# A decoder block on one core: setup merged, values shared by all heads, low parts two tiles later, and high parts made by a multiplication with an accumulator

## The reference, cut to what matters

```python
# 1. x (1024 x 128) goes through 4 sLSTM layers, each with a small feed-forward part
def step(carry, wx_t):
    h, c, n, m = carry
    raw = wx_t + jnp.einsum('bhd,hdgo->bhgo', h, rk) + b
    ...
    hn = jax.nn.sigmoid(og) * cn / nn
_, ys = lax.scan(step, ...)          # 1024 tokens, one after the other
# 2. cross-attention: 16 heads of 64, 6404 context rows of 96 numbers
q = xn @ Wq; k = context @ Wk; v = context @ Wv
out = softmax(q k^T / 8) v @ Wo + bo
# 3. a mixture of 8 experts with one expert per token
```

## Time and profile before

| | us |
|---|---|
| three runs | 4532.09, 4542.35, 4545.08 |
| median of the runs | 4542.35 |
| the profiled execution: its own time | 4545.85 |
| the profiled execution: its span, first to last instruction | 4544.1 |
| busy: PE, DVE, ACT, POOL | 3847.7, 3629.3, 2821.0, 1054.5 |
| mean granted TensorE clock | 0.855 |

### The profile page before, as it was taken

How to read it: one execution, slowest core, us unless ns; L and a number is a source line. 1 busy time by engine, 2 the same in 40 slices (tenths; PEclk the granted TensorE clock), 3 DMA queues, 4 the chain that set the end, 5 groups by cost and what they waited for, 6 DMA issues and landing times. The chain is left out here.

```text
span 4544.1 us, 104550 instructions
## 1 busy us (share of the span) xinstructions
PE 3847.7 (85%) x37946; PEld 2067.0 (45%) x37946; DVE 3629.3 (80%) x15783; ACT 2821.0 (62%) x9013; POOL 1054.5 (23%) x1218
## 2 busy tenths in 40 slices
PE   3777777746999999999999999999958988889987
PEld 2334333333454454454454454454414555555545
DVE  4777888878888788888888888888668888878865
ACT  2555555543666666666666666666717777777774
POOL 1000000000000000000000000000028888788883
PEclk7555555555999999999999999999959999999998
DMA  2122122200000000000000000000041221222200
GB/s 64 65 71 66 65 75 70 77 6 3 3 4 3 3 4 2 4 4 2 3 2 2 4 2 2 3 2 2 3 116 38 75 75 47 66 75 58 55 23 24
DMA packets 92506, 144.25 MB, mean 32 GB/s; under 512 B 11956, under 2 KB 85492, under 8 KB 86836
## 3 DMA queue, kind: packets, MB, share of 16 engines
q1 hardware_dynamic: 91988, 137.57, 10.8%
HBM read 80.56 MB, written 55.77 MB: 30 GB/s over the span
## 5 line engine op out<-in xcount | busy, mean ns | idle before, releaser
L1270 PEld LDWEIGHTS G<-st,rec_w 128*128 128x128 f16 x19456 | 608.8, 100 | 895.5 <-DVE st L1430 856.5
L1694 POOL TENSOR_TENSOR plt<-pft,pht 128x512 f16<-128x512 f32 x765 | 876.5, 1171 | 241.6 <-DVE pht L1932 164.6
L1270 PE MATMUL G<-st,rec_w 128*128 128x1 f16 x19456 | 683.8, 165 | 287.5 <-DVE st L1430 268.4
L1222 PE MATMUL OA<-pf,vals 128*97 128x512 f32 (+1 forms) x1632 | 852.5, 603 | 0.7
L1166 ACT ACTIVATE st<-hb 32x16 f16<-32x16 f32 x1216 | 258.9, 213 | 704.4 <-DVE hb L1425 703.8
L267 DVE TENSOR_REDUCE mx<-MT 128x1 f32<-128x512 f32 (+1 forms) x832 | 521.1, 661 | 93.6 <-PE MT L1747 89.8
L1689 ACT ACTIVATE pft<-ST,ln_prob 128x512 f32<-128x512 f32 (+1 forms) x816 | 540.9, 687 | 68.0 <-PE ST L1769 67.7
L1146 ACT ACTIVATE pf<-SC,ln_prob 128x512 f32<-128x512 f32 (+1 forms) x816 | 560.7, 687 | 20.5
L267 DVE TENSOR_REDUCE mx<-MB 128x1 f32<-128x512 f32 (+1 forms) x832 | 537.6, 660 | 43.5 <-PE MB L259 29.0
L1687 ACT ACTIVATE pht<-ST,ln_prob 128x512 f16<-128x512 f32 x510 | 350.9, 688 | 262.0 <-PE ST L1769 256.5
L1157 ACT ACTIVATE tf<-G 32x16 f32<-32x16 f32 x1216 | 213.0, 175 | 356.9 <-PE G L1270 328.6
(11 more groups left out here) (365 smaller groups left out, 7259.8 us busy)
## 6 DMA issues: line engine op xcount, KB each, us to landing
vc<-scr_v SPq DMA_DIRECT2D x16, 1644.8 KB, 15.8
kc<-scr_k SPq DMA_DIRECT2D x32, 816.0 KB, 12.7
scr_v<-v_hl SPq DMA_DIRECT2D x24, 1032.0 KB, 5.6
scr_k<-k_hl SPq DMA_DIRECT2D x192, 128.0 KB, 1.7
k<-scr_k SPq DMA_DIRECT2D x16, 816.0 KB, 6.7
w<-in_L_ffn_W SPq DMA_DIRECT2D x16, 256.0 KB, 4.7
xin<-x SPq DMA_DIRECT2D x38, 48.0 KB, 1.8
scr_v<-v_hl SPq DMA_DIRECT2D x2, 774.0 KB, 5.2
```

The lines of the kernel that those rows point to most:

```text
L1222: pe.matmul(OA[0:at.DC + 1, :], at.vals[0:rows, i, :], pf[0:rows, tile % 2, :], start=(i == 0), stop=(i == KT - 1)).then_inc(pv_done, 1)
L1270: mm = pe.matmul(g[:, t, c:c + 1], rec_w[:, c, :], st[:, c:c + 1], start=False, stop=(c == C - 1), skip_group_check=True)
L1694: return eng.tensor_tensor(pl[0:k, t % NP_, :], pf[0:k, t % NP_, :], ph[0:k, t % NP_, :], ALU.subtract)
```

## The change

1. `attention_prepare` is gone. The loads of the attention's inputs are issued by ACT, in front of its other work, inside the sLSTM's setup block; the turning of the context and the splitting into `keys_h` and `keys_l` are done in that block too, after the sLSTM's weights. The order of SP's loads is changed, some waits are made narrower (`d_ln` for two small weights instead of `d_w` for all), and the turned sLSTM weights have two PSUM banks instead of one.
2. The per-head products `qk_w` and `vo_w` (three steps a head: `turn`, `qk`, `vo`), the doubled query weights `wq_d` and the split of the context into 16-bit values, `vals_c`, stand in the first recurrent stage, at places 3, 5, 6, 9, 23 (products), 27 (queries) and 29 (split) of a chunk.
3. The per-head values are gone, with their 102 items, their 26 stores and the loads of the tail. The keys' 104 items stand at 11 places of a chunk.
4. The tail uses the shared values: 4 x 193 columns for a high part, 4 x 97 for a low part. `o_n`, `o_low`, `o_t` get 96 or 97 columns a head instead of 64 or 65, and the output product takes `vo_w`.
5. In the tail the low part of tile *t* is multiplied two tiles later (`LATE = 2`), and at the end of a head the last three one after the other; the ring of `pft`, `pht` and `plt` has 8 places instead of 6.
6. DVE makes a high part by `tensor_scalar` (times 1.0, plus 0.0) with `accum_out`, whose sum nothing reads, instead of `tensor_copy`.

```diff
-class ByHead:
-    PLACES = (0, 1, 2, 3, 4, 5, 7, 8, 11, 12, 13, 14, 15, 18, 19, 20, 21, 25, 28, 30, 31)
+class WeightsByHead:
+    PLACES = (3, 5, 6, 9, 23)
+    T_SPLIT, SPLIT_TILES, T_QUERY = 29, 6, 27
+class KeysByHead:
+    PLACES = (0, 2, 4, 7, 8, 11, 12, 15, 18, 19, 21)
...
@@ the setup block, ACT
-                    a.wait_ge(d_w, 16 * (12 + L))
+                    a.dma_start(at.wk_sb[:, :], wa["Wk"]).then_inc(d_wk, 16)
+                    a.wait_ge(c_zero, 1)
+                    a.dma_start(ctx_f[0:at.LAST, KT - 1, 0:at.DC], ctx_in[full:at.NK, :]).then_inc(d_ctx, 16)
+                    a.dma_start(ctx_f[:, 0:KT - 1, 0:at.DC], ...).then_inc(d_ctx, 16)
+                    for dst, src in (wq_sb, wv_sb, wo_sb, post_w):
+                        a.dma_start(dst, src).then_inc(d_att, 16)
...
+                    for j in range(0, KT, 4):
+                        a.wait_ge(k_t, j // 4 + 1)
+                        s.activation(at.keys_h[...], KP[j // 4 % 4][...], ACT.Copy, scale=at.C_SCALE).then_inc(k_hi0, 1)
+                    s.activation(at.vals[:, :, 0:at.DC], ctx_f[:, :, 0:at.DC], ACT.Copy, scale=at.C_SCALE)
+                    a.wait_ge(d_w, 16 * N_W)
                     for l in range(L):
                         s.activation(up_w[:, l, :], up_w[:, l, :], ACT.Copy, scale=ln2_w[:, l:l + 1])
@@ the setup block, DVE
-                    dve.wait_ge(d_w, 16 * (12 + L))
+                    dve.wait_ge(d_ln, 32)
...
+                    v.tensor_tensor(at.wk_l[:, :], at.wk_sb[:, :], at.wk_h[:, :], ALU.subtract)
+                    for j in range(0, KT, 4):
+                        keys_low(j)
+                    dve.wait_ge(d_w, 16 * N_W)
@@ the first recurrent stage, ACT
+                            if weights and n - 1 in weights.at_step:
+                                what, h = weights.at_step[n - 1]
+                                if what == "turn":
+                                    a.wait_ge(w_turn, h + 1)
+                                    s.activation(at.w_turned[:, h % 2, :], MB[0][...], ACT.Copy).then_inc(w_turned, 1)
+                                ... qk, vo alike, from MB[1]
+                            if weights and n - 1 in weights.split:
+                                s.activation(at.vals_c[:, j0:j1, 0:at.DC], at.vals[:, j0:j1, 0:at.DC], ACT.Copy).then_inc(v_hi, 1)
@@ the tail, PE
-    NS, NP_, NK_ = 3, 6, 3
+    NS, NP_, NK_, LATE = 3, 8, 3, 2
-    VC = 2 * DHEAD + 1
+    VC = 2 * DC + 1
...
                         pe.matmul(OA[i // 2][:, (i % 2) * 256:(i % 2) * 256 + VC], ph[0:k, t % NP_, i * P:(i + 1) * P],
-                                  vc[0:k, g % 2, j, :], ...)
+                                  at.vals_c[0:k, j, :], ...)
                     if t + NS < TOTAL:
                         scores(t + NS)
-                    (wait for the low part of t, four matmuls of 65 columns)
+                    if j >= LATE:
+                        values_low(t - LATE)
+                    if j == KT - 1:
+                        for u in range(t - LATE + 1, t + 1):
+                            values_low(u)
@@ the tail, DVE
-                        v.tensor_copy(ph[0:k1, (t + 1) % NP_, :], pf[0:k1, (t + 1) % NP_, :]).then_inc(h_dve, 1)
+                        v.tensor_scalar(ph[0:k1, (t + 1) % NP_, :], pf[0:k1, (t + 1) % NP_, :], 1.0, 0.0, ALU.mult, ALU.add,
+                                        accum_out=high_sum[0:k1, (t + 1) % NP_:(t + 1) % NP_ + 1]).then_inc(h_dve, 1)
```

More of the change, by code:

```diff
@@ L427, in __init__ @@
         assert len(self.load) == len(self.store) == len(ends)
-class ByHead:
-    PLACES = (0, 1, 2, 3, 4, 5, 7, 8, 11, 12, 13, 14, 15, 18, 19, 20, 21, 25, 28, 30, 31)
+class WeightsByHead:
+    PLACES = (3, 5, 6, 9, 23)
+    T_SPLIT, SPLIT_TILES, T_QUERY = 29, 6, 27
+    def __init__(self, at, chunks, chunk_steps):
+        steps = [("turn", "qk", "vo")[i % 3] for i in range(3 * at.HEADS)]
+        places = [c * chunk_steps + p for c in range(chunks) for p in self.PLACES]
+        assert len(steps) <= len(places) and chunks * self.SPLIT_TILES >= at.KT
+        self.at_step = {s: (what, i // 3) for i, (s, what) in enumerate(zip(places, steps))}
+        self.split = {c * chunk_steps + self.T_SPLIT: (c * self.SPLIT_TILES, min((c + 1) * self.SPLIT_TILES, at.KT))
+                      for c in range(chunks) if c * self.SPLIT_TILES < at.KT}
+        self.query = {c * chunk_steps + self.T_QUERY: (2 * c, 2 * c + 2) for c in range(at.HEADS // 2)}
@@ L449, in in_chunk @@
-    def in_chunk(self, chunk, late):
-        return [i for s, i in self.at_step.items()
-                if s // self.chunk_steps == chunk and (s % self.chunk_steps >= self.T_STORE) == late]
-def slstm_stage(nc, x, w, scratch_in, scratch_out, dims, at, first_row, xa_out, keys_out, values_out):
+        self.pieces = [(c * 512, min(c * 512 + 512, at.KT * P)) for c in range(-(-at.KT * P // 512))]
+        total = at.HEADS // 2 * len(self.pieces)
+        places = [c * chunk_steps + p for c in range(chunks) for p in self.PLACES]
@@ new lines, in __init__, with item, before_store, after_store @@
+        assert total <= len(places)
+        self.at_step = {s: i for i, s in enumerate(places[:total])}
+        self.total = total
+    def item(self, i):
+        pair, c = divmod(i, len(self.pieces))
+        return pair, *self.pieces[c]
+    def before_store(self, chunk, chunk_steps):
+        return [i for s, i in self.at_step.items() if s // chunk_steps == chunk and s % chunk_steps < self.T_STORE]
+    def after_store(self, chunk, chunk_steps):
+        return [i for s, i in self.at_step.items() if s // chunk_steps == chunk and s % chunk_steps >= self.T_STORE]
@@ L489, in sem @@
             return s
[L492 removed]
+        ident = at.identa
         gate_w = sb("gate_w", [P, L, H, 4, Q])
@@ L1595, in attention_tail @@
         d_k2 = [sem(f"d_k2{i}") for i in range(2)]
-        d_vc = [sem(f"d_vc{i}") for i in range(2)]
         uses = ["turn", ("q", 0), ("q", 1), ("row", 0)]
```

436 lines of the change are left out of this document (172 added, 264 removed).

## The result

| | before | changed |
|---|---|---|
| median of the runs | 4539.14 (4532.09 to 4545.08, 4 runs) | 4428.56 (4419.72 to 4438.11, 4 runs) |
| profiled execution, span | 4545.85, 4544.1 | 4419.72, 4418.0 |
| up to the first recurrent step | 122.87 | 67.60 |
| first recurrent stage | 805.6 | 768.6 |
| second recurrent stage | 2362.8 | 2354.2 |

The ratio is 0.9757, with a 95% interval of 0.9731 to 0.9784: 110.6 us faster. The forecast was 4449 and the range 4400 to 4505. Between the two profiled executions the difference is larger, 126.1 = 55.3 + 37.0 + 8.6 + 1.2 + 25.8 - 1.7. I had put these terms at 59, 29, 0, 0, 6 and 0.

What follows compares the result with a forecast made beforehand. PE was taken to set the tail, though not alone, and the setup to start waiting for loads. Setup -59, first stage -29 and tail -6 made -94 from 4545.85: 4451.9, forecast 4449 after the 3.5 over the median, range 4400 to 4505.

Steps and rivals of the forecast that it cites:

- Setup: Up to the first recurrent step: one merged block replaces two, first step at 63 instead of 122.87, -59 (range -48 to -66).
- First stage: First recurrent stage: fewer items beside the chain, a chunk 77.6 instead of 80.5, -29 over ten (range -8 to -50).
- Second stage: Second recurrent stage: same instructions before and now, put at nothing.
- Tail: Attention tail: 0 for the 15 heads with maxima beside them, -6 for the last head.
- the width: Tail: wider matmuls add 8.2 us of PE work a head, 130 over 816 tiles, absorbed by PE's waits.
- LATE: Tail: low part two tiles later, so PE's 46.4 us idle for POOL's low part should go nearly all.
- the accumulator: Tail, DVE's high part: 0.72 each instead of the cast's 0.82, -30 us of DVE's busy time over 16 heads.
- The last head: Tail's end, without maxima beside it: 60 us instead of 66.16, -6.
- A: Tail: PE's waits are links of one ring, each widening adds straight, +131; 4589, or 4585 after the 3.5; chance 5%.
- B: Loads hold the setup (-48), chunks give only -18, 1.3 a head stays in the tail (+20): 4496; chance 18%.
- C: Tail: with LATE and no lock PE's waits shrink to about 4 a head, heads 63.9, -51: 4404; chance 17%.
- D: Tail: the accumulator form waits for POOL as the cast did, 1.10 each, +55: 4503; chance 7%.

Runs made afterwards that it cites:

- narrow: Tail forms with 129 columns for a high part, 65 for a low; the changed kernel made so from a head's second tile on: 4376.81, ratio 0.9646, tail 994.8.
- wide: Tail forms with the shared values' 193 and 97 columns; the changed kernel with low part at once and cast again: 4470.44, ratio 0.9855, tail 1086.1.

## Why the prediction was right, and where it was not

- **Setup**, -59 forecast, -55.3 measured. The mechanism and the order of the chain were right. The loads of the gate weights were mis-sized by 4.6 us (22.63 against 18), which is the whole of the first step's 67.6 against 63; what stands behind them came out right in sum, and DVE has no wait for `gn_w`.
- **First stage**, -29 forecast, -37.0 measured. That the cost goes by place was right (places 28 and 30 cost 0.8 to 0.97 each, shown by moving items there), but I gave the products a cost they mostly don't have. Of their places only 9 costs much, 0.4 to 0.6 a chunk. A chunk of 76.9 lies within the 2 us of the forecast's 77.6 that I had allowed.
- **Second stage**, 0 forecast, -8.6 in the profiles. No effect of the change is shown: it lasts 2359.0 to 2364.2 in the four profiles with the old setup and 2346.9 to 2371.0 in the ten with the new one (below).
- **Tail**, -6 forecast, -25.8 measured. The sum is 20 us off, its terms by more. I had the width at 0 since PE's waits would absorb it. In the old order that nearly holds, 17.3 of 130 (two more buffers included). In the new one it costs 49.9 (1042.9 against 993.0): the same change that brought the gain took the waits away in which the width was to hide. I used the slack twice, once for the wider matmuls and once for LATE. And I had the accumulator at nothing but -30 us of DVE's busy time, where it alone brings 45.1 in the old tail and 32.3 in the new one; LATE, which I had only as what takes up the width, brings 27.8 in the new one. The errors, +50 for the width and some -70 for LATE and the accumulator together, cancel but for -20. That they do, and that the total so lies near the forecast, is luck and not the mechanism that I had.
- The last head, forecast 60, took 4336.17 - 4276.63 = 59.5. The other heads took (4276.63 - 3355.58) / 14 = 65.8, forecast 67. One sign did not hold: POOL's wait for DVE's `pht` was to be well under 164.6 and is 156.9. The starts of DVE's reads of the sums, of which these are the differences, answer to the earlier trace rows.
- **Rivals.** A (each widening adds straight) is excluded: the width costs 17.3 to 56.8 us between the narrow and the wide row of the same order, not 131. B is excluded as a whole: the setup gave 55.3 and not 48, the chunks 37.0 and not 18, and the tail fell. C (PE's own work becomes the bound) came about in part: PE is busy 97% of the time, but a head takes 65.8 and not 63.9. D is excluded: the accumulator form never exceeds 0.69 us, and its read 0.09. The page "SBUF — State Buffer" of the Trainium skill, section Who interferes with whom, has this form outside the lock, and the spread of 666 to 689 ns agrees; what that is worth in this tail only the experiments above show.

By these numbers the shared values don't pay in these two stages: they cost 50 us in the tail, and the first stage, where 102 items went and the products came, is 37 shorter. It wasn't tried to run the new tail and the merged setup with per-head values, so whether that would be faster than the changed kernel is open.

In the table LATE and the accumulator overlap with narrow matmuls (-50.4 and -45.1 alone, -75.8 together) and help each other with wide ones (-10.9 and -15.4 alone, -43.2 together). Part of this is TensorE's clock. In the tail the granted clock falls to its lower level for short stretches: for 38.2 us in all in the kernel before, 23.9 with the accumulator, 30.0 with LATE, 21.0 with both; with wide matmuls 29.2 with neither, 37.5 with the accumulator, 32.1 with LATE, 13.6 in the changed kernel. What a stretch costs can be read where two executions of the same tail differ in one. Windows at the change from the fourth head to the fifth (columns as above), of the changed kernel and then of the kernel with three items at the chunk's end, whose tail is the same program:

```profile
3552.00:3556.00 4.00, 2.93 (x32) 1.82 (x30) 2.90 (x8) 2.42 (x5) 2.39 (x3) 1.00 0.99 222
3556.10:3559.50 3.40, 3.40 (x14) 1.73 (x12) 1.48 (x5) 1.79 (x3) 2.30 (x2) 0.50 0.95 192
```

```profile
3563.00:3567.00 4.00, 2.93 (x31) 1.83 (x30) 2.88 (x8) 2.45 (x5) 2.42 (x3) 1.00 1.00 222
3567.10:3570.50 3.40, 3.40 (x28) 2.11 (x27) 2.45 (x6) 3.01 (x5) 2.78 (x3) 1.00 1.02 207
```

PE had waited 1.07 us at the head's change in both; the clock fell in one, and the fifth head took 66.7 us there against 65.1. That is 1.6 us for a stretch of 3.4. At this price, an estimate, some 12 of the tail's 25.8 us go with the clock. With it taken out the wide forms nearly add (-12 for LATE and -19 for the accumulator alone, -36 together), and the overlap of the narrow ones stays (-46 and -38 alone, -67 together). Whether a form has few stretches by itself or by chance is open: of the six kernels with the changed tail five have 14 us of them and one has 20, but each other form was profiled once. Why the narrow forms overlap is open too.

## What to carry to other kernels

Slack can be spent once. Where a change fills an engine's waits and also removes them, price the filling in the state after the removal, or write the combinations as a table and measure its corners. A short operation with a wide spread in its group (405 to 1815 ns) is worth more attention than its share of busy time says: making it even, at almost the same mean (0.82 against 0.76), gave 45 us in the kernel before.

## What the runs showed that I had not expected

TensorE's granted clock falls for short times in the second stage, at places that differ between executions of the same work. A window of the kernel before, and one of the changed kernel around the same recurrent steps (columns as above):

```profile
1660.00:1676.00 16.00, 15.73 (x123) 9.80 (x124) 8.71 (x44) 6.86 (x25) 0.00 (x0) 0.57 0.02 5
```

```profile
1566.00:1578.00 12.00, 11.25 (x127) 7.09 (x127) 9.67 (x50) 7.67 (x29) 0.00 (x0) 1.00 0.01 2
```

0.57 is mostly the lower of its two levels (1.2 of 2.4 GHz). PE had no long pause before it: it was busy for 19.17 of the 20 us before this window, and for 18.99 of 20 before the other, where the clock stayed. At 0.57 the step from 1661.68 took 5.71 us; at 1.00 the same step took 3.70. This step and the two behind it make 5.0 of the 8.6 us between the two profiles. Over the profiles of the kernels here, with the same instructions in this stage, it lasts from 2346.9 (mean clock 0.95) to 2371.0 (0.93). That is as much as the runs of one kernel scatter, and why a difference of a few us has to be read from its own stage.

In the setup a cast of 32 x 32 numbers took 5.51 us, from 13.67 to 19.18. It ran beside a memset by POOL, and ends with it, at 19.13:

```profile
13.46 5.67 POOL L536 MEMSET keys_h<- 1x6528 f16 x1
```

It cost nothing, only because the gate weights hadn't come. In the forecast of the setup I had looked at no such meeting.
